# Two-layer cross-attention and mixture-of-experts kernel: one more pair of expert loads, an earlier down product, fewer products of zeros, two output stores

## The reference, cut to what is computed

```python
x = x + _L0_xattn_ref(_layernorm(x), ctx_768, ...)   # 16 heads, 8 batches of 100 queries, 361 keys
x = x + _L0_ffn_ref(_layernorm(x), ...)              # 8 experts, the best one of each token
x = x + _L1_xattn_ref(_layernorm(x), ctx_768, ...)   # 8 heads, a null key, stable layer norm
x = x + _L1_ffn_ref(_layernorm(x), ...)

def _L1_ffn_ref(hidden_states, router_w, e_bias, Wg, Wu, Wd, SWg, SWu, SWd):
    ...
    topk_idx, topk_w = _route(x, router_w, e_bias)   # 8 of 64 experts, out of 4 of 8 groups
    coef = jnp.zeros((T, E), topk_w.dtype).at[jnp.arange(T)[:, None], topk_idx].add(topk_w)
    g = jnp.einsum('th,ehi->tei', x, Wg)
    u = jnp.einsum('th,ehi->tei', x, Wu)
    h = jax.nn.silu(g) * u * coef[:, :, None]
    moe_out = jnp.einsum('tei,eih->th', h, Wd)
    shared = jax.nn.silu(x @ SWg) * (x @ SWu) @ SWd
    return (moe_out + shared).reshape(orig_shape)
```

## Time and profile before

| | |
|---|---|
| median of 3 runs | 664.12 us (662.41 to 664.93) |
| the profiled execution, its own time | 664.93 us |
| its span, first instruction to last | 663.3 us |
| PE busy | 618.9 us, 93% |
| DVE, ACT, POOL busy | 382.7, 402.7, 305.4 us |
| DMA | 71.20 MB, mean 107 GB/s |

### The profile page before, as it was taken

One profiled execution on the slowest core, in us unless ns is written; L12 is line 12 of the kernel. 1 busy time (PEld: TensorE's weight loads), 2 busy tenths in 40 slices (PEclk: granted clock), 3 DMA queues, 4 the chain that ended last, 5 costly groups with the idle time before them and its releaser, 6 DMA issues.

```text
span 663.3 us, 15407 instructions
## 1 busy us (share of the span) xinstructions
PE 618.9 (93%) x4808; PEld 502.8 (76%) x4809; DVE 382.7 (58%) x1205; ACT 402.7 (61%) x973; POOL 305.4 (46%) x486
## 2 busy tenths in 40 slices
PE   7999899999988999998999989999899799999996
PEld 6998566666677999876878756666656798999995
DVE  2533667777761111138898755666576466666663
ACT  4545899989953443245767697786551455555553
POOL 4223555558645000011010003777415688888883
PEclk9999999999968999999999999999998799999998
DMA  6138700005343995112120020000034867677744
GB/s 161 51 96 276 265 2 2 2 2 194 108 138 108 309 326 170 32 37 81 36 57 2 1 54 2 1 1 1 2 99 95 228 185 185 180 187 194 194 114 115
DMA packets 71884, 71.20 MB, mean 107 GB/s; under 512 B 10740, under 2 KB 65298, under 8 KB 71702
## 3 DMA queue, kind: packets, MB, share of 16 engines
q1 hardware_dynamic: 63484, 59.62, 29.4%
q0 software_dynamic: 4816, 8.07, 5.8%
q10 hardware_dynamic: 3530, 2.82, 1.5%
HBM read 55.18 MB, written 15.31 MB: 106 GB/s over the span
## 4 chain that ended last, share of the span: by engine, by line
PE 67%; ACT 11%; DVE 8%; issue 5%; DMA 4%; POOL 3%; ACTq 0%; SPq 0%; DVEq 0%; POOLq 0%
PE psum L1399 6%; PE psum L1388 6%; ACT probs L911 4%; PE psum L1890 3%; PE psum L1912 3%; PE psum L1899 3%; PE psum L2541 3%; PE psum L2543 3%; PE psum L2542 3%; PE psum L1938 2%; PE psum L837 2%; PE psum L827 2%; DMA x_rows<-xc_dram,slot_rows 1%; PE psum L1673 1%; POOL probs L977 1%
## 5 line engine op out<-in xcount | busy, mean ns | idle before, releaser
L911 ACT ACTIVATE probs<-probs,negmax 100x361 f32<-100x361 f32 x128 | 68.9, 587 | 10.6 <-POOL probs L977 10.5
L990 DVE TENSOR_SCALAR_CACHE_REDUCE probs<-psum 100x361 f32<-100x361 f32 x128 | 60.6, 530 | 17.2 <-PE psum L827 17.2
L837 PEld LDWEIGHTS psum<-ident,probs 100*128 100x128 f32 (+1 forms) x384 | 38.0, 151 | 25.2 <-issue 16.7
L837 PE MATMUL psum<-ident,probs 100*128 100x100 f32 (+1 forms) x384 | 45.9, 255 | 10.8 <-ACT probsT L919 4.0
L977 POOL TENSOR_SCALAR probs<-probs 100x722 f32<-100x722 f32 x64 | 50.5, 788 | 5.1
L1429 ACT ACTIVATE kT_all<-psum,kT_all 128x128 f32<-128x128 f32 x88 | 25.0, 369 | 42.5 <-PE psum L1388 42.5
L2541 PE MATMUL psum<-xT_high,we_high 128*128 128x400 f32 x128 | 45.6, 357 | 3.4 <-DVE v_all L2794 3.4
L2543 PE MATMUL psum<-xT_high,we_low 128*128 128x400 f32 x128 | 45.1, 352 | 0.0
L2542 PE MATMUL psum<-xT_low,we_high 128*128 128x400 f32 x128 | 45.1, 352 | 0.0
L2712 POOL TENSOR_TENSOR we_low<-v_all,we_high 128x512 fp32r<-128x512 f32 (+1 forms) x34 | 40.0, 1309 | 10.6 <-ACT we_high L2630 10.1
L1388 PEld LDWEIGHTS psum<-kT_all,v_all 128*128 128x128 f32 x352 | 40.6, 192 | 4.9 <-issue 4.6
(11 more groups left out here) (473 smaller groups left out, 1801.7 us busy)
## 6 DMA issues: line engine op xcount, KB each, us to landing
v_all<-in_L_ffn_W_dram SPq DMA_DIRECT2D x16, 1024.0 KB, 5.5
xs_dram<-zeros SPq DMA_DIRECT2D x1, 7424.0 KB, 23.5
kT_all<-coefT_dram SPq DMA_DIRECT2D x16, 400.0 KB, 4.3
v_all<-in_L_ffn_Wg_dram SPq DMA_DIRECT2D x32, 128.0 KB, 2.4
v_all<-in_L_ffn_Wu_dram SPq DMA_DIRECT2D x32, 128.0 KB, 2.9
v_all<-in_L_ffn_Wd_dram SPq DMA_DIRECT2D x32, 128.0 KB, 3.1
ctx_nat<-in_ctx_dram SPq DMA_DIRECT2D x16, 192.0 KB, 2.4
kT_all<-xs_dram ACTq DMA_DIRECT2D x13, 128.0 KB, 3.2
```

Of the source, the lines that this page charges most:

```text
L837: last = nc.tensor.transpose(pT_ps[0:rows[t], t, hh * NQ:(hh + 1) * NQ], probs[:, n % NPB, hh, t * P:t * P + rows[t]], ident[0:NQ, 0:NQ])
L911: last = nc.scalar.activation(row, row, ACT.Exp, bias=negmax[:, n % NPB, hh:hh + 1])
L990: last = nc.vector.tensor_scalar(probs[:, n % NPB, hh, 0:NKV], psum[0:NQ, n % 2 * 2 + hh, 0:NKV], -CLAMP, None, ALU.max, ALU.max, accum_ou ...
```

## The change

Eight edits, all in the last step:

1. Three products of zeros in place of five behind the router logits.
2. `load_gate_up(1)` stands ahead of SP's wait for `coefT_stored` and of `load_coef(0, 0)`, in place of behind them.
3. SP's loop loads in the last pass too (`2 * i < total`): two more dense and two more small experts, by the entries of the lists behind the last used one, with their rows of weights and ranks. What is loaded is split, and not used further.
4. The two additions to `we_loaded` that stood in place of those loads are gone; SP waits for the extra coefficient and rank loads behind the load of `x`.
5. `down(0, 0)` stands ahead of the counts in place of behind the list.
6. The six products of zeros ahead of the loop are gone.
7. ACT waits for the extra small and down weights ahead of its last copies.
8. Two stores of four batches each, in place of four of two.

```diff
-        for _ in range(5):
+        for _ in range(3):
             nc.tensor.matmul(psum[:, 5, 0:D], zeros[:, 0:P], zeros[:, :], start=True, stop=True)
...
+        load_gate_up(1, dense[1])
         sp.wait_ge(coefT_stored, 16)
         load_coef(0, 0, dense[0])
-        load_gate_up(1, dense[1])
         load_down(1, dense[1])
...
-                    with sp.If(2 * i + 2 < total):
+                    with sp.If(2 * i < total):
                         dense = [load(i + 1, p) for p in range(2)]
...
-        for p in range(2):
-            sp.wait_ge(we_loaded[p], 16 * total)
-            sp.sem_inc(we_loaded[p], 32)
         for k in range(2):
             sp.wait_ge(rows_added[k], 8 * total)
         sp.dma_start(x[:, 1:B + 1, :], sum_dram[0:B * NQ, :].rearrange("(b q) d -> q b d", b=B)).then_inc(x_loaded[0], 16)
+        for p in range(2):
+            sp.wait_ge(coef_loaded[p], 8 * total + 16)
+            sp.wait_ge(rank_loaded[p], 8 * total + 16)
         sp.wait_ge(rows_added[0], 8 * total + 16)
...
+        down(0, 0)
         pe.wait_ge(sh_taken, 5)
         pe.wait_ge(route_step, 1)
...
-        down(0, 0)
         pe.sem_inc(gu_in_psum, 8)
...
-        pe.wait_ge(route_taken, 2)
-        for _ in range(6):
-            nc.tensor.matmul(psum[:, 3, 0:D], zeros[:, 0:P], zeros[:, :], start=True, stop=True)
...
+        for k in range(2):
+            act.wait_ge(ws_loaded[k], 24 * total + 48)
+        for p in range(2):
+            act.wait_ge(wd_loaded[p], 8 * total + 16)
...
-            for k in range(4):
-                sp.wait_ge(x_final, k + 1)
-                two = slice(2 * k, 2 * k + 2)
-                sp.dma_start(a["out"][two].rearrange("b q d -> q b d"), x[:, 1 + two.start:1 + two.stop, :]
+            for k in range(2):
+                sp.wait_ge(x_final, 2 * k + 2)
+                half = slice(k * B // 2, (k + 1) * B // 2)
+                sp.dma_start(a["out"][half].rearrange("b q d -> q b d"), x[:, 1 + half.start:1 + half.stop, :]
                              ).then_inc(out_stored, 16)
-            sp.wait_ge(out_stored, 64)
+            sp.wait_ge(out_stored, 32)
```

## The result

| | median | range | runs |
|---|---|---|---|
| before | 663.07 us | 661.77 to 665.73 | 10 |
| after | 668.79 us | 666.63 to 671.85 | 10 |

The ratio is 1.0086 (95% interval 1.0062 to 1.0109): the change makes the kernel 5.7 us slower, 4.1 to 7.2 by the interval. The forecast was 664.6 us, no change, with a range that ended at 667.7. It was wrong: the time lies beyond the range. The profiled execution of the changed kernel took 669.29 us, its span was 667.6.

A forecast was written before the change was run, and what follows sets the result against it. PE was taken to bound the kernel, with 67% of the chain, setting the pace through the loop. Head -3.5, extra loads +3.3 and two stores +0.7 gave +0.5 us on the 664.12 median: 664.6 us, range 661.0 to 667.7.

The forecast's parts named there:

- What bounds the kernel: Whole launch: PE sets the pace from 526 to 652; gains ahead of the loop arrive one for one, losses behind are paid fully.
- Extra loads: Last pass: extra loads occupy SP's queue, so the load of `x` is issued 4.0 us later; 3.3 us lost.
- about 0.7 us of the 4.0 are covered: End: DVE's additions were released by PE, so 0.7 us of the later `x` load is hidden and 3.3 are not.
- The upper bound, 4.5: End: largest loss from the extra loads, if `x` also shares its queue with the large coefficient load just ahead.
- The gate and up load passes the wait: Ahead of the loop, edit 2: load issued 2.25 us earlier, landing at 513.2, PE restarting at 516.9; 3.5 us won.
- lower bound of 2.25: Ahead of the loop: the gain in us from the earlier gate and up load if it takes 5.0 us to land.
- Edits 1, 5 and 6 at nothing: Ahead of the loop: fewer zeros counted 0; moved down product uses 0.4 us of cover, stores weights 1.3 us earlier.
- Two stores: End, edit 8: same bytes and rate, but the first byte waits for a second addition; 0.7 us lost.
- The fallen clock: Rival, chance 0.09: PE's clock falls earlier, near 484 to 486; counts, list and loads slip 1 to 2 us; 665.6 to 666.6.
- The early load lands no earlier: Rival, chance 0.15: gate and up load waits for bytes, lands at 515.5, gain 1.2 us; 666.9, or 668.1 with upper end bound.
- The held clock: Rival, chance 0.16: PE's clock stays at 1.00 in the first pass after shorter idling; 662.8 us.
- `x` in time: Rival, chance 0.12: load of `x` is not late, the 3.3 us shrink to 1 or less; 661.3, or 659.5 with held clock.

The follow-up runs named there:

- mean of six against seven: Profile means: six kernels with edits 2, 5 and 6, the changed kernel among them, against seven with before's head; closing products 155.1 against 156.7 us after the picks.
- the kernel with the late load: Kernel before plus one SP wait for PE's closing product ahead of the last load of `x`, no load added: 1.0101 (1.0063 to 1.0138), 6.7 us slower.

## Why the prediction was wrong, point by point

| step | forecast | timed | in the profiles |
|---|---|---|---|
| head (edits 1, 2, 5, 6) | -3.5 | -1.8 and -2.5 | -1.6, mean of six against seven |
| extra loads (3, 4, 7) | +3.3 | +5.5 (3.7 to 7.3) | +4.6 |
| two stores (8) | +0.7 | +2.0 (0.1 to 3.8) | +1.2 |
| sum | +0.5 | +5.7 and +5.0 | +4.2 |

The mechanisms were those named, and every one was mis-sized in the same direction. Only for the extra loads is the miss clear of noise in the timing: 3.3 lies below 3.7, the low end. The interval of the two stores holds their 0.7, and of the two timings of the head one holds its 3.5 (1.8 is 0.5 to 3.1, 2.5 is 0.7 to 4.3); there the profiles carry the finding.

- *What bounds the kernel* stood. A gain ahead of the loop reached its end nearly whole (1.6 of 1.9 us, on the means), and a loss behind it was paid in full (5.9 us for 5.3 us of delay in the kernel with the late load).
- *Extra loads.* "The data are not needed, but SP's queue is" was right, and so was the 4.0 us for the changed kernel: issue relative to the closing products moved from -4.8 to -0.8. With these edits alone it moved by 4.6. The step that failed is "about 0.7 us of the 4.0 are covered". That cover was read from bytes that stop flowing, by the forecast at 655.5, and a first addition at 656.44. The row itself has bytes until about 655.8 (67 GB/s in the slice from 655.6), so even that was 0.3 too early. And the load was not usable when its bytes stopped: where the load itself releases the additions, they start 7.0 to 7.5 us after the issue, which for 649.30 is 656.3 at the earliest. Cover: at most 0.2, and not 0.7. In the changed kernel the late load also took 7.8 us rather than 7.1; with edits 3, 4 and 7 alone it took 7.1, and there SP was later. The cost was 4.6 us in both profiles. The upper bound, 4.5, nearly met that; the timed 5.5 lies above it, but the interval holds both.
- *The gate and up load passes the wait.* The direction was right, and 3.5 was too much. The issue gained 0.9 instead of 2.25, because the profile of before had been taken in a head where SP was 2 us quicker than in most; the landing gained 1.4, as forecast (5.0 to 3.7). The forecast also had the coefficients ready 1 us ahead of DVE's multiply. In the changed kernel they came last: the multiply could have run 0.5 us behind ACT's silu at 516.1, as before, and ran at 517.39, 0.8 later. With these the term fell below its lower bound of 2.25.
- *Edits 1, 5 and 6 at nothing.* For edit 1 that holds within 0.35%, the upper end of its interval, and the clock fell with it in other kernels. Edits 5 and 6 were not run alone; beside edit 2 they bring 1.0 to 2.1 us by the ratios (0.9968 and 0.9952 against 0.9983), and nothing by the profiles, and the intervals hold both. That is open.
- *Two stores.* First byte one addition later: right, 0.7. The upper bound, 1.0, was passed even in the profile, by 0.5 us of slower flow at the start, while the first store was alone in the queue.
- *Rivals.* The fallen clock came (it had 0.09) and was almost wholly covered, not at the 1 to 2 us that it was priced at. "The early load lands no earlier" was half true: it landed earlier but DVE then waited for the coefficients behind it, and with 4.5 lost at the end its upper figure, 668.1, was the nearest number of all to 668.8. That is luck in part: it had the head gain 1.2 us, and the timings have 1.8 and 2.5. The held clock was seen in one kernel of the new head (PE at 1.00 from 518 to 526, edits 2, 5 and 6, second run, though at 0.67 from 512 to 516), whose closing products still came 154.4 us after the picks, in the middle of its kind. `x` in time did not happen.

The range failed with the sum. Three terms were taken as independent with bounds of about 1 us each, yet all three had been read from the same single profile, at its most favourable in the head and at a tie in the end. Even the three worst bounds together, -2.25 + 4.5 + 1.0, give 667.4 us, below the 668.8 measured.

## What to carry to other kernels

A load that nobody needs still costs what stands behind it in the issuing queue. Here about 5 us went into the place of one issue, and the traffic of the extra dense loads cost nothing that could be measured: guard such loads, or issue the one that ends the kernel first. When a profile names one releaser, ask how far behind the next one was, and count as landed only what a waiting engine has shown to be landed. Read a gain of 2 us from several executions, not from one.

## What the runs showed of the hardware that I had not expected

- SP's issue of one DMA in the head took 0.41 us in the profile of before (the row at 504.37 of line 2232 has 405 ns) and 1.76 us in the changed kernel. Over all profiles it took 0.41 us in five and 1.46 to 1.95 in nine, with and without the new head. The lines of 2267 on SP, before and then after:

```profile
L2267 SPq TENSOR_LOAD <-n_used x1: 270/270/270, 506.0 to 506.0; - x1
```

```profile
L2267 SPq TENSOR_LOAD <-n_used x1: 1326/1326/1326, 506.4 to 506.4; - x1
```

- Leaving the loop cost SP 2.1 us between its last coefficient load (through at 649.67) and the load of `x` (651.74), in which it issued nothing; with edits 3, 4 and 7 alone it was 2.5 us.
- With the same instructions up to there and the same 0.85 us of idling, TensorE's clock fell to half in one kernel (edits 1, 2, 5 and 6, second run) and not in another (edit 1 alone).
- A store of 100 rows kept 0.57 to 0.67 of the DMA engines busy, one of 96 rows up to 0.86, for 226 against 254 GB/s at best.
